# A table-driven recommendation kernel: its order of work, its transfers of factors and GpSimd's shares set anew

## The reference

```python
def _L0_rec_ref(embeddings, W0, W1, W2):
    x0 = embeddings                       # 512 x 32 fields x 16
    xk = x0
    outs = []
    for W in (W0, W1, W2):
        xk = jax.nn.relu(jnp.einsum('bmd,bhd,mhk->bkd', x0, xk, W))
        outs.append(jnp.sum(xk, axis=2))
    return jnp.concatenate(outs, axis=1)
...
h = jnp.concatenate([z, dense_ctx], axis=1)
h = jnp.maximum(h @ W_top1 + b_top1, 0.0)
h = jnp.maximum(h @ W_top2 + b_top2, 0.0)
y = h @ W_top3
```

## Time and profile before

| | |
|---|---|
| median of three runs | 339.63 us |
| span of the profiled execution | 356.2 us |
| busy in the span: PE, DVE | 314.8 us, 282.1 us |
| busy in the span: POOL, ACT | 246.0 us, 53.3 us |
| granted TensorE clock, mean | 0.990 |
| HBM read and written | 55.55 MB, 2.03 MB |

### The profile page before, as it was taken

How to read it: one execution, slowest core, us unless ns; L and a number is a source line. 1 busy time by engine, 2 the same in 40 slices (tenths; PEclk the granted TensorE clock), 3 DMA queues, 4 the chain that set the end, 5 groups by cost and what they waited for, 6 DMA issues and landing times.

```text
span 356.2 us, 4290 instructions
## 1 busy us (share of the span) xinstructions
PE 314.8 (88%) x1602; PEld 114.9 (32%) x1602; DVE 282.1 (79%) x172; ACT 53.3 (15%) x77; POOL 246.0 (69%) x195
## 2 busy tenths in 40 slices
PE   0378588988699788898999999998999999999997
PEld 0344224432222223332333333332333333333334
DVE  0039477869499878999999999999998879999220
ACT  1000011012020221110112120121022111220011
POOL 5646566766367668869997987896998569729300
PEclk9999989999899999999999999999999999999999
DMA  6272853834875982979499989683699897050000
GB/s 183 65 231 72 230 154 73 230 71 110 295 240 174 326 292 65 326 217 280 167 317 289 296 284 297 201 268 67 215 346 337 290 291 194 17 133 2 0 0 0
DMA packets 34302, 68.09 MB, mean 191 GB/s; under 512 B 5866, under 2 KB 15082, under 8 KB 34282
## 3 DMA queue, kind: packets, MB, share of 16 engines
q1 hardware_dynamic: 23562, 56.80, 49.0%
q10 hardware_dynamic: 6624, 9.96, 9.4%
q0 software_dynamic: 4096, 1.06, 3.5%
HBM read 55.55 MB, written 2.03 MB: 162 GB/s over the span
## 4 chain that ended last, share of the span: by engine, by line
PE 59%; POOL 16%; issue 11%; DVE 9%; another core or an unknown queue 2%; DMA 1%; DVEq 1%; ACT 0%; POOLq 0%; SPq 0%
PE acc L1060 37%; PE acc L1055 12%; POOL gathered L719 10%; DVE vz L805 8%; POOL pz L746 6%; PE factor L984 2%; PE factor L1093 2%; PE factor L1021 1%; PE factor L1088 1%; PE acc L1050 1%; PE factor L998 1%; PE acc L1082 1%; PE factor L1100 1%; DVEq L800 1%
## 5 line engine op out<-in xcount | busy, mean ns | idle before, releaser
L805 DVE TENSOR_TENSOR vz<-fields_sb,factor 128x1024 f32<-128x1024 f32 (+3 forms) x113 | 230.5, 2090 | 20.7 <-PE factor L984 7.6
L1060 PE MATMUL acc<-vz,w_sb 128*64 128x512 f32 (+1 forms) x800 | 172.6, 569 | 10.9 <-DVE vz L805 3.6
L719 POOL DMA_INDIRECT gathered<-in_table,index x128 | 121.6, 950 | 65.0 <-issue 31.5
L746 POOL TENSOR_TENSOR pz<-fields_sb,hidden 128x1024 f32<-128x1024 f32 (+1 forms) x52 | 117.9, 2292 | 19.4 <-DMA hidden<-relu_out 9.6
L1060 PEld LDWEIGHTS acc<-vz,w_sb 128*64 128x64 f32 x800 | 57.8, 139 | 113.7 <-issue 98.6
L1055 PE MATMUL acc<-vz,w_sb 128*64 128x512 f32 x216 | 60.9, 621 | 3.7 <-DVE vz L805 2.9
L1060 PE MATMUL acc<-pz,w_sb 128*64 128x512 f32 x192 | 48.1, 594 | 0.3 <-POOL pz L746 0.3
L934 ACT ACTIVATE relu_out<-acc 128x512 f32<-128x512 f32 (+1 forms) x30 | 15.3, 512 | 126.3 <-PE acc L1060 47.3
L890 ACT ACTIVATE factor<-hidden 128x1024 f32<-128x1024 f32 (+1 forms) x23 | 20.1, 878 | 65.8 <-DMA hidden<-relu_out 34.3
L805 DVE TENSOR_TENSOR vz<-rotated,factor 128x2048 f32<-128x2048 f32 x12 | 26.9, 2279 | 1.8 <-issue 1.8
L1055 PEld LDWEIGHTS acc<-vz,w_sb 128*64 128x64 f32 x216 | 16.4, 139 | 36.4 <-issue 24.6
(11 more groups left out here) (44 smaller groups left out, 83.2 us busy)
## 6 DMA issues: line engine op xcount, KB each, us to landing
fields_sb<-fields SPq DMA_DIRECT2D x48, 512.0 KB
rotated<-fields SPq DMA_DIRECT2D x24, 512.0 KB
fields_sb<-fields SPq DMA_DIRECT2D x32, 256.0 KB
hidden<-relu_out ACTq DMA_DIRECT2D x30, 256.0 KB, 5.6
own<-fields SPq DMA_DIRECT2D x6, 512.0 KB
gathered<-in_table,index POOLq DMA_INDIRECT x128
hidden<-relu_out ACTq DMA_DIRECT2D x16, 128.0 KB
fields<-gathered SPq DMA_DIRECT2D x6, 256.0 KB, 5.2
```

The source lines that it names most:

```text
L719: nc.gpsimd.indirect_dma_start(gathered[:, pair % GRING, j, :], None, table, bass.IndirectOffsetOnAxis(ap=index[:, i:i + 1], axis=0)).then ...
L746: nc.gpsimd.tensor_tensor(pz[:, at % PRING, 0:cols], fields[s][:, t, col:col + cols], hidden_of(step, g), ALU.mult).then_inc(pz_ready, 1)
L805: nc.vector.tensor_tensor(vz[:, at:at + nt, 0:cols].rearrange("p t (a n) -> p t a n", n=half), src[:, t:t + nt, col:col + cols].rearrange( ...
L1060: last = nc.tensor.matmul(acc_of(step, ab), w_sb[layer][:, kt, :], z[:, ab * half:(ab + 1) * half], start=start and j == 0, stop=stop and ...
```

## The change

Only tables of numbers change. BEGUN moves (0,4) ahead of (1,3) and (2,6) ahead of (0,8). PAIRED keeps (1,3) alone of seven steps. Of the wide steps (1,9) leaves SPREAD, and (2,4) and (2,7) leave HALF, so that their factors go wholly by DMA; of the narrow ones (2,0), (2,1) and (1,3) now stand in SPREAD and (1,1) in HALF. GpSimd makes 7 narrow tiles (4 before) and 47 wide ones (48 before), shared otherwise among the steps. Gathers, their waits and one pair of loads are set anew.

```diff
-BEGUN = [..., (2, 2), (1, 3), (0, 4), (0, 5), ..., (1, 7), (0, 8), (2, 6), (2, 7), ...]
+BEGUN = [..., (2, 2), (0, 4), (1, 3), (0, 5), ..., (1, 7), (2, 6), (0, 8), (2, 7), ...]
...
-SPREAD = [(1, 0), (2, 3), (1, 4), (1, 5), (1, 9)]
+SPREAD = [(1, 0), (2, 0), (2, 1), (1, 3), (2, 3), (1, 4), (1, 5)]
...
-HALF = [(2, 0), (1, 2), (2, 2), (1, 3), (2, 4), (1, 7), (2, 7)]
+HALF = [(1, 1), (1, 2), (2, 2), (1, 7)]
...
-POOL_TILES = {..., (1, 4): 1, (1, 5): 5, ..., (1, 7): 3, (2, 6): 4, (2, 7): 5, (1, 8): 6, (1, 9): 4, (2, 8): 3, (2, 9): 6}
+POOL_TILES = {..., (1, 4): 0, (1, 5): 3, ..., (1, 7): 4, (2, 6): 5, (2, 7): 6, (1, 8): 3, (1, 9): 5, (2, 8): 4, (2, 9): 6}
...
-FIRST_GATHERS = 21
+FIRST_GATHERS = 24
-GATHERS_IN = {..., (1, 5): (10, 0, 0, 2, 0), ...}
+GATHERS_IN = {..., (1, 5): (19, 0, 0), ...}
...
-PACED = {12: 1, 13: 2, 14: 4, ..., 126: 105, 127: 106}
+PACED = {11: 1, 12: 1, 13: 1, ..., 126: 93, 127: 98}
...
-PAIRED = [(2, 0), (1, 1), (1, 2), (2, 1), (2, 2), (1, 3), (2, 3)]
+PAIRED = [(1, 3)]
...
-LOADS = [..., ('fields', 6), ('fields', 7), ('scratch', 8), ('operands', 8), ...]
+LOADS = [..., ('fields', 6), ('scratch', 8), ('fields', 7), ('operands', 8), ...]
```

More of the change, by code:

```diff
@@ L58, in turn @@
     return sum(1 for a in range(b) if stream(a) == stream(b))
-BEGUN = [(0, 0), (1, 0), (0, 1), (2, 0), (0, 2), (1, 1), (0, 3), (1, 2), (2, 1), (2, 2), (1, 3), (0, 4), (0, 5),
-    (2, 3), (1, 4), (1, 5), (2, 4), (0, 6), (2, 5), (0, 7), (1, 6), (1, 7), (0, 8), (2, 6), (2, 7), (0, 9), (1,
-    8), (1, 9), (2, 8), (2, 9)]
+BEGUN = [(0, 0), (1, 0), (0, 1), (2, 0), (0, 2), (1, 1), (0, 3), (1, 2), (2, 1), (2, 2), (0, 4), (1, 3), (0,
+    5), (2, 3), (1, 4), (1, 5), (2, 4), (0, 6), (2, 5), (0, 7), (1, 6), (1, 7), (2, 6), (0, 8), (2, 7), (0,
+    9), (1, 8), (1, 9), (2, 8), (2, 9)]
 INSIDE = {}
@@ L71 @@
 BURST = (1, 2, 3)
-SPREAD = [(1, 0), (2, 3), (1, 4), (1, 5), (1, 9)]
-HALF = [(2, 0), (1, 2), (2, 2), (1, 3), (2, 4), (1, 7), (2, 7)]
-POOL_TILES = {(1, 0): 0, (2, 0): 0, (1, 1): 1, (2, 1): 0, (1, 2): 0, (2, 2): 0, (1, 3): 0, (2, 3): 3, (1, 4): 1,
-    (1, 5): 5, (2, 4): 3, (2, 5): 4, (1, 6): 4, (1, 7): 3, (2, 6): 4, (2, 7): 5, (1, 8): 6, (1, 9): 4, (2, 8): 3,
-    (2, 9): 6}
-FIRST_GATHERS = 21
[L85 to L90, removed]
[5 rows of a table removed]
-BEHIND_SPREAD = {10: 1, 11: 3, 15: 4, 24: 5, 26: 6, 36: 7, 43: 8, 45: 9, 55: 10, 61: 11, 80: 12, 85: 13, 93: 14}
+SPREAD = [(1, 0), (2, 0), (2, 1), (1, 3), (2, 3), (1, 4), (1, 5)]
+HALF = [(1, 1), (1, 2), (2, 2), (1, 7)]
+POOL_TILES = {(1, 0): 0, (2, 0): 0, (1, 1): 2, (2, 1): 1, (1, 2): 0, (2, 2): 0, (1, 3): 0, (2, 3): 4, (1, 4):
+    0, (1, 5): 3, (2, 4): 3, (2, 5): 4, (1, 6): 4, (1, 7): 4, (2, 6): 5, (2, 7): 6, (1, 8): 3, (1, 9): 5, (2,
+    8): 4, (2, 9): 6}
+FIRST_GATHERS = 24
+GATHERS_IN = {(0, 1): (1,), (0, 2): (5,), (1, 1): (3, 4), (0, 3): (5,), (2, 1): (11,), (0, 4): (10,), (0, 5):
+    (15,), (2, 3): (1, 0, 1, 0), (1, 5): (19, 0, 0), (2, 4): (5, 0, 0), (0, 6): (6,), (2, 5): (2, 0, 0, 4),
+    (0, 7): (4,), (1, 6): (0, 1, 1, 0), (1, 7): (1, 1, 1, 0), (2, 6): (3, 0, 0, 0, 0)}
+PACED = {11: 1, 12: 1, 13: 1, 14: 1, 15: 2, 16: 3, 17: 3, 19: 5, 21: 5, 22: 5, 24: 6, 25: 6, 26: 9, 29: 9, 30:
[6 rows of a table added]
+BEHIND_SPREAD = {17: 1, 26: 5, 29: 5, 60: 5, 68: 9, 70: 9, 99: 11, 105: 11, 113: 11}
 AFTER_ROW = (8,)
-PAIRED = [(2, 0), (1, 1), (1, 2), (2, 1), (2, 2), (1, 3), (2, 3)]
+PAIRED = [(1, 3)]
 TURN_LEAD, TURN_STEP = 4, 1
@@ L120 @@
 LOADS = [('scratch', 0), ('fields', 0), ('scratch', 1), ('operands', 1), ('fields', 1), ('scratch', 2),
[L121 to L124, removed]
+    ('operands', 2), ('scratch', 3), ('operands', 3), ('fields', 2), ('scratch', 4), ('operands', 4),
+    ('fields', 3), ('scratch', 5), ('operands', 5), ('fields', 4), ('fields', 5), ('scratch', 6), ('operands',
+    6), ('scratch', 7), ('operands', 7), ('fields', 6), ('scratch', 8), ('fields', 7), ('operands', 8),
+    ('scratch', 9), ('operands', 9), ('fields', 8), ('fields', 9)]
 OWN, ACROSS = -1, L0TILES
```

## The result

The changed kernel took **343.98 us**, the median of four runs (341.77, 342.43, 345.53, 346.21), against 339.54 for the kernel before (339.00 to 340.64): a ratio of 1.0137, 95% interval 1.0077 to 1.0197. It is 1.4% slower; 335.2 was forecast, with a range to 341.

A forecast was written before the change was run, and what follows sets the result against it. Bound: VectorE's idle time before 141 us, then VectorE and TensorE both full. Steps 1 to 6, -1.6, -1.8, -1.0, +1.5, +1.9 and -3.4, sum to -4.4 from 339.6: 335.2 us, range 329 to 341.

The forecast's parts named there:

- Step 1: Narrow stage: GpSimd makes 7 narrow tiles instead of 4, sparing VectorE three at 536 ns: -1.6 us.
- the prediction's own sign of being wrong: VectorE before 141 us: new idle time of over 4 us would show the prediction wrong.
- step 2: Put of (0,5) ahead of the fold: VectorE's 1.84 us wait goes, -1.8; 0 if own or rotated data come late.
- Step 4: New VectorE wait at (2,3), whose spread needs fold, join and relu of (1,3): +1.5 us, ends 0 and +4.3.
- Step 3: Six of seven joins and folds go from the chain to the relu: -1.0 us, ends 0 and -6.1.
- Rival A: Joins: step 3's idle time is real in the runs and all goes, -6.1 instead of -1.0: 330.1 us, chance 0.18.
- Step 5: (1,4) to (0,7): three wide tiles move to VectorE, +3.2, less the 1.26 us wait for (1,4)'s spread: +1.9 us.
- Step 6: From (0,7), TensorE full: spreads of (2,7), (1,9), 1.07 us each, and 1.32 idle before oz of (0,8) go: -3.4 us.
- Rival B: GpSimd becomes the bound from (2,3) to (0,7): no change, 339.6 us, chance 0.22.
- Rival C: New relays land late, VectorE stands at (2,4), (1,8) and (1,9): slower, 346.9 us, chance 0.13.
- L: Relay time from relu to end of first put; beyond 12.7 us (2,4) and (1,9) lose; 15.1 makes it 0.5% slower.

The follow-up runs named there:

- second profile: The kernel before, unchanged, profiled once more: 339.28 us, span 338.4 us, where the first profiled execution had 356.2.
- run 5: Changed kernel, narrow products kept, GpSimd's gathers in the narrow stage dealt out anew: 339.38 us.
- run 11: Kernel of run 5 with (1,3) ahead of (0,4) again: 337.46 us.
- run 4: Kernel before with six of its seven joins and folds gone, (1,3) keeping its own, nothing else: 337.54 us.
- run 8: Kernel of run 4 with (0,4) moved ahead of (1,3), nothing else: 340.35 us.
- mended kernel: Changed kernel with gathers dealt anew (run 5, 339.38 us); for run 13 also with (1,3) ahead of (0,4) again (run 11, 337.46 us).
- run 15: Kernel of run 4 with the join of (1,3) dropped too, so no join at all: 335.64 us.
- run 6: Kernel of run 4 with the change's wide shares alone, gathers ahead of the given-up products moved to the next ones: 341.13 us.
- run 13: Kernel of run 11 with TensorE's spreads back for (1,9) and the first halves of (2,4) and (2,7): 338.85 us.
- run 9: Kernel of run 4 with (2,6) ahead of (0,8), last eight gathers, shares from (1,7) on and new load order, without the change's relays: 353.95 us.
- run 14: Kernel of run 11 with three wide tiles of (1,4) and (1,5) back on GpSimd, gathers there about as before, old load order: 344.71 us.
- run 3: Changed kernel with TensorE's spreads back for (1,9) and the first halves of (2,4) and (2,7): 344.48 us.
- run 2: Changed kernel with four gathers moved from ahead of GpSimd's second product of (1,1) to (0,3): 343.30 us.
- run 7: Kernel of run 4 with the change's relays alone, (1,9), (2,4) and (2,7) without spreads: 342.30 us.

## Why the prediction was wrong

**The basis.** The sum was made on an execution 16.6 us longer than the runs, and the difference was set aside as holes somewhere. They lay in the first stage, on the waits that the prediction took for the kernel's idle time: 27.5 us of VectorE there. In the second profile about the same work, from 22 us to the first unit of (1,4) at 125.3, takes 103.3 us with VectorE busy for 91.2, so it idles 12.1.

**Step 1** failed, and decides the result. "GpSimd idles there often enough to take them": it did idle, but ahead of a product that waits for its operand, and what counts is when a product is due, not how much idle time there is. The sum put at nothing the wait of TensorE for a late narrow product, and with it the new places of the gathers in this stage: forecast -1.6, and in the changed kernel 3.82 us of TensorE at (1,1), 3.71 and 2.17 of VectorE behind it, which is the prediction's own sign of being wrong (over 4 us of new idle time). With seven gathers moved the whole program is 4.6 us shorter (run 5). The price of the products was near: with the gathers dealt anew the end of (2,3) is 1.8 us earlier than in the kernel before without six joins (124.2 in run 11, 125.9 in run 4), though the narrow spreads differ there too. The narrow products alone, on the gathers of before, were not run.

**Steps 2 and 4** together were -0.3 and cost 2.8 alone (run 8) and 1.9 in the mended kernel (run 11). The wait at (0,5) was real and went, but the rotated data were late next, an end that step 2 had named; and the chain behind the join at (1,3) had lost a cover. Step 4 put that at 1.5; the wait at the spread of (2,3) is 1.05 in run 8, 0.89 in the changed kernel and 2.41 in run 5, and in run 8 two more waits of 1.87 stand behind it, with GpSimd late too. In the order of before the wait at (0,5) goes when the one join that the change keeps is dropped (run 15).

**Step 3** had the sign and the place, and half the size: -1.0 forecast, -1.9 measured (run 4). Rival A's 6.1 were not in the runs. The Trainium skill (Perfetto Trace Analysis, Tensor Engine Instruction) says that a matmul's end is computed, not observed; by that rule the hole behind the join would have been work. The second profile has 0.03 us there, so it was that execution's.

**Step 5** came near by luck: 1.9 forecast, 2.3 and 2.4 in the traces (run 6 and the change). It was 3.2 for three tiles less the 1.26 us ahead of (1,4), and the second profile has no such wait; so 3.2 was too much, and why is open.

**Step 6** had half the size: -3.4 forecast, -1.7 in the trace. The two spreads, 2.1 of it, were right in mechanism; 1.1 to 1.4 us are kept (run 13), as the relay of (1,9) gives some back. The other 1.3, the idle time ahead of oz of (0,8), had nothing to win. It too belongs to the first execution; in the second profile TensorE does not stand there:

```profile
229.43 1.13 PE L984 MATMUL factor<-relu_out,unit_sb 32*128 32x512 f32 x4
230.49 1.08 PE L1050 MATMUL acc<-oz,w0c_sb 128*64 128x256 f32 x8
```

The base of run 9 has no such idle time either, so its expectation rests on one that only run 6 shows.

**Rival B**, GpSimd as the bound from (2,3) on, was to give no change. Its times held: in the changed kernel the first product of (1,5) ends 26.0 us after the last of (2,3), where it had 26.2, and that costs TensorE 0.71 us (150.78), not the whole gain. In run 14, with three wide tiles more, GpSimd is late. **Rival C** named the relays and a price near the result (346.9), but its cause is not the change's: with the spreads back it stays as slow (run 3), and in the mended kernel the relays are the faster form (run 13). Its condition was close at (1,9) alone. There VectorE had the factor in time with L = 274.20 - 265.44 = 8.8 us in the changed kernel and stood 2.26 us with 277.70 - 265.93 = 11.8 in run 2, so about 9.5 us were covered, not 12.7: VectorE had run ahead of a full TensorE, whose relu comes late. The Trainium skill (DMA: Bandwidth & Descriptors, Issuing engines are not separate DMA queues) says that DMAs share the same 16 engines and interleave, whichever engine issues them. From this the prediction worked out that L would be near 19.5; no row shows the 8.3 us in that estimate, and the longest relay of the changed kernel took 10.2 (relu at 180.77, end of the first put at 191.01).

**What stays open:** why the changed kernel's runs scatter by 4.4 us. Its wait at (1,1) differs from execution to execution (3.82 us in its profile, 4.47 in run 3, with half clock behind both), but run 11, which has no such wait, scatters as much (335.67 to 340.13), and run 15 hardly at all (335.45 to 335.75). What the rest of the 2.1 us of run 6 after (0,7) is, beyond the 1.22 at oz of (0,8), was not tried either, nor what lengthened the first profiled execution.

## What to carry to other kernels

Compare the span of the profiled execution with the times of the runs before reading a single wait; where they differ by 5%, a stall is not known to be the kernel's until a second profile shows it. Before work moves to an engine that has idle time, follow its list up to each product and ask when that product is due: seven gathers in the wrong place cost 4.6 us here. Tables that order one program are not independent: an order of loads needed the gathers that came with it, and relays the order of steps, so a part is to be judged on both kernels.

## What the runs showed of the hardware that was not expected

Behind an idle time of TensorE of 2.85 to 4.5 us in the first stage the granted clock fell to 1.2 GHz, half of 2.4 GHz, for a while. In run 2 it is 0.63 from 84 to 91 us, behind 2.85 us of idling; in the changed kernel 0.91 in the stretch from 52 to 72 us, behind 3.82; in run 3 0.83 there, behind 4.47. In run 7, behind 3.87 us, twelve matmuls took 5.39 us (granted clock 0.56 from 246.2 to 253 us):

```profile
246.28 5.39 PE L1060 MATMUL acc<-vz,w_sb 128*64 128x512 f32 x12 [3.87 <-DVE vz L805]
```

where twelve such matmuls take 2.79 us at the full clock (run 6):

```profile
125.98 2.79 PE L1060 MATMUL acc<-vz,w_sb 128*64 128x512 f32 x12 [0.93 <-DVE vz L805]
```

It is no rule for every such idle time: in run 14 the four matmuls behind 3.03 us took 1.98 us, those behind 3.06 us the 1.08 of the full clock (granted clock 1.00 from 180.6 to 186 us). So a late product can cost its wait and, as in run 7, two thirds as much again.

Two profiles of one kernel differ by 17.8 us in span (356.2 and 338.4), with the same instructions in the same order on all four engines; why is open.
